# One combined first transfer, a new written-out order of steps, and half of the last V spread issued by ScalarE, in a two-block transformer kernel

## The chip, the core and the metric

One NeuronCore of a Trainium2 chip runs the whole kernel. It has five engines with a queue each: TensorE (PE in the profile; PEld is its weight load), VectorE (DVE), ScalarE (ACT), GpSimd (POOL) and SyncE (SP), which here only issues transfers. The metric is device microseconds of one execution, as a median over runs.

## What is computed

The reference runs two blocks one after the other on x of 32 batches x 32 tokens x 128 features, all in fp32:

```
cmod = silu(c) @ w_ada + b_ada        # 6 blocks: shift, scale, gate; twice
x_mod = ln(x) * (1 + scale) + shift;  k, q, v = split(x_mod @ w_qkv)
w = softmax(q k^T / 8) per head (16 heads of 8);  x = x + gate * (w v @ w_proj + b)
x = x + gate2 * (gelu(x_mod2 @ w_mlp1) @ w_mlp2)          # layer 0, "mlp"
self = [x, q] @ W_self.T ;  label bias and penalty from adj (32 x 32 x 11 labels)
for d in (0, 1):  out += gat_attention(self, adj or adj^T)  # 16 heads, first 20 tokens as keys
return x + relu(self + out)                                # layer 1
```

## The kernel before

Tokens lie in 8 groups of 4 batches (128 rows). Layer 0 normalises and projects in five chunks (`CHUNKS`: groups 0; 1; 2-3; 4-5; 6-7), and everything behind it goes in four halves of 2 groups (`MIDS`). Attention goes by unit: 8 units of layer 0 (one per group) and 16 of layer 1 (group x direction; units 8 to 23). A unit passes these steps: `scores` (32 small products on TensorE), `badd` (layer 1: the bias, VectorE, L1503), `max` (L1513, L1517), `sub` (L746, L1528; for odd units of layer 1 on GpSimd), `turn` (transposes, L1167, L1170), `exp` (ScalarE, L1307, L1310), `values` (products with V, L1190, L1199), and for a pair of units `recip` and `mult` (VectorE, L1541, L1552). Layer 1 ends with `ya`, `yb`, `relu` (L755, L766, L1562) and `store`.

The order of all work is a list written out by hand or by a planner beforehand: `ORDER` holds 541 entries (stage, key). `ON` and `TAKE_ON` say which engine runs an entry; each engine runs its own entries strictly in the order of the list, and waits on semaphores for what an entry reads. `take` copies a product out of PSUM. `BANKS` gives every product its PSUM bank, and an entry also waits until the bank's last user has been read (`bank_freed`, L699). An attention unit keeps its scores in one of 4 slots, so `badd` of a unit waits for `turn` of the unit four places before it (L1504).

Places that the change and the prediction touch:

- Loads (`fetch`, L833). SP issues `cols` (51 small columns: the condition, the biases), x1, `ada0` (blocks 0 and 1 of w_ada), qkv, x2, x3, x4, `ada1` (blocks 2 to 5) and the rest; ACT issues x0. `HOLD` makes a fetch wait until another has landed (`ada1` for `ada0`).
- Start. `warm` are products of ones with ones on TensorE that no one reads: 8, then 3 more behind `cmod 0`. `silu` (L1276) reads `cols`, `cmod 0` (L1026) reads silu's result and `ada0`. `masks` on VectorE reads `ident` of GpSimd; `plus1` on GpSimd reads `cols`.
- ScalarE loads a table when its function changes between Exp and Gelu. In the old order all 16 takes of `mlp1` (Gelu, L1239) lie between `exp` of unit 6 and `exp` of unit 11.
- `spread ('v1', m)` (L898): V of half m goes by 8 SBUF to SBUF transfers to the layout that `values` wants, all issued by SP. `values` waits for all 8.

Of the kernel before, what the change touches and what calls it, by code (L numbers as in the profile page):

```python
# [152 lines left out]
BANKS = {('warm', ('w0', 8)): 0,  # L153
 ('cmod', 0): 4,
 ('warm', ('w1', 3)): 5,
 ('xnT', 0): 0,
# [44 lines left out]
 ('turn', 7): 2,
 ('bias', 0): 3,
 ('bias', 1): 3,
 ('yT', 0): 1,
# [1 line left out]
 ('x1tok', 0): 1,
 ('xn2T', 0): 4,
 ('mlp1', 0, 0): 1,
 ('mlp1', 0, 1): 6,
# [1 line left out]
 ('mlp1', 0, 3): 6,
 ('mlp2', 0): 6,
 ('self', 0): 5,
 ('selfT', 0): 5,
 ('x2tok', 0): 2,
 ('k1', 0, 0): 2,
 ('q1', 0, 0): 0,
 ('k1', 0, 1): 7,
 ('q1', 0, 1): 2,
 ('v1', 0, 0): 6,  # L220
 ('v1', 0, 1): 3,
# [10 lines left out]
 ('yT', 1): 2,
 ('proj', 1): 2,
 ('x1tok', 1): 4,
 ('xn2T', 1): 2,
 ('mlp1', 1, 0): 2,
 ('mlp1', 1, 1): 2,
# [1 line left out]
 ('mlp1', 1, 3): 7,
 ('mlp2', 1): 2,  # L240
 ('self', 1): 1,
 ('selfT', 1): 1,
 ('x2tok', 1): 1,
 ('k1', 1, 0): 3,
 ('q1', 1, 0): 3,
 ('k1', 1, 1): 0,
 ('q1', 1, 1): 2,
 ('v1', 1, 0): 1,
 ('v1', 1, 1): 2,
# [1360 lines left out]
```

How the kernel before makes its waits and increments, by code:

```python
        def shift(engine, name, p):  # L721
            g0, g1 = MIDS[p]
            bs = slice(g0 * UB, g1 * UB)
            for s in fresh(name, ("take", (("xn2T", p), 0)), ("take", (("cmod", 1), 0))):
                engine.wait_ge(*s)
            return engine.tensor_tensor(xm[:, bs, :], xm[:, bs, :], over_s(cmod, 3, bs), ALU.add)
# [1 line left out]
        def resid(engine, name, which, m):  # L728
            g0, g1, bs = batches("mid", m)
            if which == 1:
                for s in fresh(name, ("xb", 0), ("take", (("proj", m), 0))):
                    engine.wait_ge(*s)
            else:
                for s in fresh(name, ("resid1", m), ("take", (("mlp2", m), 0)), ("dense", ("x1tok", m))):
                    engine.wait_ge(*s)
            return engine.tensor_tensor(xT[:, bs, :], gated[:, bs, :], xT[:, bs, :], ALU.add)
# [1 line left out]
        def subtract(engine, name, n):  # L738
            if layer_of(n):
                for s in fresh(name, ("badd", n), ("max", n)):
                    engine.wait_ge(*s)
            else:
                for s in fresh(name, ("copy", n), ("max", n)):
                    engine.wait_ge(*s)
            e = e_of(n)
            return engine.tensor_tensor(e, e, nm_of(n).unsqueeze(2).broadcast_to(list(e.shape)), ALU.add)
# [1 line left out]
        def add_dirs(engine, name, g):  # L748
            n = UNITS.index((1, 1, g))
            for s in fresh(name, ("mult", pair_of(n)), ("mult", pair_of(UNITS.index((1, 0, g))))):
                engine.wait_ge(*s)
            if g in SELF_FIRST:
```

## Time and profile before

| | us |
|---|---|
| median of 3 runs | 91.72 (91.64 to 93.18) |
| the profiled execution, its own time | 91.11 |
| its span, first to last instruction | 89.4 |
| PE busy | 79.5 (89%) |
| DVE busy | 68.4 (76%) |
| POOL busy | 57.7 (65%) |
| ACT busy | 51.1 (57%) |

Busy time of an engine is a share of the whole span; which engine holds the end up differs by stretch. In the chain of work that ended last PE has 72%, DVE 13%, POOL 5% and issue 5%. The granted TensorE clock was 0.989 of full speed as a mean, and 1.00 in every stretch read below.

### The profile page before, as it was taken

The numbers are of one execution on the slowest core, as the hardware profiler recorded it, in microseconds if no ns is written. First come the engines' busy times: TensorE is split into PE (matmuls) and PEld (weight loads), VectorE is DVE, ScalarE is ACT, GpSimd is POOL, SyncE is SP. The second block draws the span as 40 slices with busy tenths as digits, with TensorE's granted clock in tenths as the row PEclk, the third lists the DMA queues.
The fourth block names the chain that finished last, engine by engine and source line by source line (L and its number), as shares of the span: only waits on it lengthen the run. The fifth ranks groups of instructions, "written<-read, shape, count | busy, mean of one in ns | idle before, by whom it ended". The sixth has DMA issues, their size and how long they took to land.

```text
span 89.4 us, 4174 instructions
## 1 busy us (share of the span) xinstructions
PE 79.5 (89%) x1768; PEld 61.0 (68%) x1768; DVE 68.4 (76%) x203; ACT 51.1 (57%) x114; POOL 57.7 (65%) x82
## 2 busy tenths in 40 slices
PE   5997999998999899999999999999989969976810
PEld 5997757655666777878987766778777746645700
DVE  0679899799798865779262699299979997898870
...
GB/s 25 242 235 187 248 223 226 310 209 214 127 29 65 166 22 0 0 0 7 0 0 31 40 23 0 17 53 16 13 15 50 29 6 8 46 33 73 0 141 42
DMA packets 7076, 7.08 MB, mean 79 GB/s; under 512 B 1169, under 2 KB 6193, under 8 KB 7057
## 3 DMA queue, kind: packets, MB, share of 16 engines
...
## 4 chain that ended last, share of the span: by engine, by line
PE 72%; DVE 13%; issue 5%; POOL 5%; ACT 1%; DVEq 0%; POOLq 0%; ACTq 0%
PE ps_all L1155 11%; PE ps_all L1076 8%; PE ps_all L1082 8%; PE ps_all L1056 6%; PE ps_all L1000 6%; PE ps_all L1167 5%; PE ps_all L1119 4%; PE ps_all L1170 4%; PE ps_all L1104 4%; PE ps_all L1106 3%; PE ps_all L1199 2%; PE ps_all L1190 2%; DVE E L1503 2%; PE ps_all L1109 2%; PE ps_all L1064 2%
## 5 line engine op out<-in xcount | busy, mean ns | idle before, releaser
L1307 ACT ACTIVATE PT<-ps_all 120x384 f32<-120x384 f32 x16 | 7.5, 489 | 7.3 <-PE ps_all L1167 7.3
L785 POOL TENSOR_TENSOR Kb<-k_raw,head_mask 128x640 f32<-128x640 f32 x4 | 5.0, 1253 | 7.0 <-ACT Kb L1256 4.3
L1239 ACT ACTIVATE hidden<-ps_all,cols 128x256 f32<-128x256 f32 x16 | 7.1, 475 | 3.7 <-PE ps_all L1076 3.7
L1076 PE MATMUL ps_all<-xm,w_rest_sb 128*128 128x256 f32 x32 | 9.1, 387 | 0.0
L966 POOL TENSOR_TENSOR rstd<-var_eps,minus_half 128x2 f32<-128x2 f32 (+1 forms) x9 | 6.0, 665 | 4.7 <-DVE var_eps L1344 4.5
L736 POOL TENSOR_TENSOR xT<-gated,xT 128x256 f32<-128x256 f32 x8 | 5.8, 729 | 4.9 <-DVE gated L1391 3.9
L746 POOL TENSOR_TENSOR E<-E,neg_max 128x320 f32<-128x320 f32 x8 | 6.1, 771 | 3.5 <-DVE neg_max L1513 3.5
L1167 PE MATMUL ps_all<-ident,E 128*120 128x128 f32 x48 | 8.1, 284 | 0.2
L1056 PE MATMUL ps_all<-xm,w_qkv_sb 128*128 128x256 f32 (+1 forms) x30 | 7.5, 360 | 0.5 <-DVE xm L1371 0.5
L1190 PE MATMUL ps_all<-Vz,PT 120*32 120x54 f32 (+1 forms) x384 | 6.2, 208 | 2.0 <-DMA Vz<-v_raw 0.9
L1190 PEld LDWEIGHTS ps_all<-Vz,PT 120*32 120x32 f32 (+1 forms) x384 | 5.2, 109 | 3.8 <-ACT PT L1307 1.3
L1082 PE MATMUL ps_all<-hidden,w_rest_sb 128*128 128x256 f32 x32 | 7.8, 386 | 0.0
L773 POOL TENSOR_TENSOR Kb<-gated,head_mask 128x1024 f32<-128x1024 f32 (+1 forms) x4 | 6.7, 1679 | 1.5 <-ACT gated L1224 1.5
L1155 PE MATMUL ps_all<-Kb,home_b 32*32 32x80 f32 x512 | 7.1, 240 | 0.7 <-issue 0.4
L1513 DVE TENSOR_REDUCE neg_max<-E 128x16 f32<-128x320 f32 x16 | 7.4, 476 | 0.2
L1256 ACT ACTIVATE Kb<-ps_all,bk_masked,head_mask 128x160 f32<-128x160 f32 x16 | 7.1, 490 | 0.7 <-PE ps_all L1106 0.7
L1517 DVE TENSOR_REDUCE neg_max<-ps_all 128x16 f32<-128x512 f32 x8 | 5.5, 691 | 1.8 <-PE ps_all L1155 1.5
L801 POOL MEMSET Vz<- 128x2592 f32 x3 | 6.8, 2257 | 0.0
L1155 PEld LDWEIGHTS ps_all<-Kb,home_b 32*32 32x32 f32 x512 | 3.9, 103 | 4.2 <-issue 2.6
L1082 PEld LDWEIGHTS ps_all<-hidden,w_rest_sb 128*128 128x128 f32 x32 | 5.9, 190 | 1.0
L1310 ACT ACTIVATE PT<-ps_all 128x512 f32<-128x512 f32 x8 | 4.5, 595 | 3.4 <-PE ps_all L1170 3.3
L746 DVE TENSOR_TENSOR E<-E,neg_max 128x320 f32<-128x320 f32 x8 | 6.2, 787 | 0.1
...
## 6 DMA issues: line engine op xcount, KB each, us to landing
...
w_rest_sb<-in_w_rest SPq DMA_DIRECT2D x1, 576.0 KB, 7.9
...
q_tok<-q_rows SPq DMA_DIRECT2D x4, 128.0 KB, 3.2
...
```

What stands on the lines that cost most here:

```text
L746: return engine.tensor_tensor(e, e, nm_of(n).unsqueeze(2).broadcast_to(list(e.shape)), ALU.add)
L801: return engine.memset(Vz1[:, m, :, :, :, :, :], 0.0)
L1056: return pe.matmul(ps[:, 0:n], w_qkv_sb[:, o:o + P], xm[:, bs, :], start=True, stop=True)
L1076: return pe.matmul(ps[:, 0:n], w_of(W_MLP1 + name[2]), xm[:, bs, :], start=True, stop=True)
L1082: ins = pe.matmul(ps[:, 0:n], w_of(W_MLP2 + j), hidden[:, slot_of(h), j, 0:n], start=(j == js[0]), stop=(j == js[-1]))
L1155: ins = pe.matmul(to[QUAD * b:QUAD * b + QUAD, j, :], qT, Kb, start=True, stop=True)
L1167: ins = pe.transpose(ps[0:KR, c * P:(c + 1) * P], E1[:, r, c * KR:(c + 1) * KR], ident[:, :])
L1190: ins = pe.matmul(ps[QUAD * b:QUAD * b + QUAD, o + c * SIX * CW:o + c * SIX * CW + w], PT[0:n, key % RING, c, b * S:(b + 1) * S], V, start ...
L1239: return act.activation(hidden[:, slot_of(h), j, 0:n], ps[:, 0:n], ACT.Gelu_apprx_tanh, bias=cols[:, R_MLP1 + j:R_MLP1 + j + 1])
L1256: return act.activation(kb1_of(h, d)[:, part, :, :], ps[:, 0:nb * M].rearrange("p (b k) -> p b k", k=M), ACT.Identity, bias=bk_masked[:, d ...
L1307: ins = act.activation(PT[0:KR, key % RING, 0:CH, :], ps[0:KR, 0:CH * P].rearrange("p (j t) -> p j t", t=P), ACT.Exp)
L1513: ins = dve.tensor_reduce(nm_of(key), e_of(key), AX.X, ALU.max, negate=True)
```

## The change

Seven edits, of which the order is by far the longest.

```diff
+V_PARTS = [[(i, i, 0, CH, 0) for i in range(HI)],
+           [(i, (i - HI) * 2 + c, c, c + 1, CH) for i in range(HI, SIX) for c in range(2)]]
-HOLD = {'ada1': 'ada0', ...
+HOLD = {'ada1': 'cols', ...
+ ('spread', ('v1', 3, 1)): 'act',
- ('fetch', 'x1'): 'sp',
- ('fetch', 'ada0'): 'sp',
+ ('fetch', 'x1'): 'act',
-        cols = sb("cols", [P, COLS])
+        first = sb("first", [P, COLS + ADA_PARTS[0][1] * P])
+        cols = first[:, 0:COLS]
-        w_ada_sb = sb("w_ada_sb", [P, 6 * P])
+        w_ada_sb = sb("w_ada_sb", [P, (6 - ADA_PARTS[0][1]) * P])
...
             if what == "cols":
-                to, of = cols[:, :], cols_dram
+                to, of = first[:, :], cols_dram
...
+        def spread(engine, name, key):
...
+            m, part = key[1:]
...
+            for i, quad, c0, c1, j in V_PARTS[part]:
+                to, of = slice(M * i, M * i + M), slice(QUAD * quad, QUAD * quad + M)
+                engine.dma_start(Vz1[to, k, i, c0:c1, 0:nb, :, :]..., v1_raw[of, j:j + c1 - c0, bs, :, :]...)
...
-                        for s in fresh("pe", ("spread", ("v1", m))):
+                        for s in fresh("pe", *[("spread", ("v1", m, part)) for part in range(len(V_PARTS))]):
```

- `cols` and the first two blocks of w_ada arrive as one transfer (25.5 + 128 KB); `ada0` is gone, `ada1` waits for the combined one, and ACT issues x1 behind x0.
- The 8 transfers of `spread ('v1', m)` become two entries of 4. SP issues them all but the second of the last half, which ACT issues.
- `warm` is 7 products in one place instead of 8 + 3.
- `BANKS` is assigned anew, and all of `ORDER` is another sequence of the same steps (543 entries). Units of layer 0 now begin with group 0. The steps' engines are the same, but for x1 and the one spread.

The new order begins so:

```diff
+ORDER = [('zero', 'ones'), ('fetch', 'x0'), ('zero', 'v0_ones'), ('ident', 0), ('masks', 0), ('fetch', 'cols'),
+         ('stats', (0, 0)), ('consts', 0), ('fetch', 'qkv'), ('plus1', 0), ('rstd', (0, 0)), ('apply', 0),
+         ('fetch', 'x1'), ('silu', 0), ('warm', ('w0', 7)), ('zero', 'vz0b'), ('dense', ('cmod', 0)),
+         ('dense', ('xnT', 0)), ('stats', (0, 1)), ('take', (('cmod', 0), 0)), ('fetch', 'x2'),
+         ('take', (('xnT', 0), 0)), ('dense', ('k', 0)), ('dense', 'vsh'), ('dense', ('v', 0)), ('dense', 'qb'),
...
```

The long list is easier read by engine. These are entries of single engines, taken out of `ORDER` in their sequence, where the prediction speaks of them:

```
SP, start     before  cols x1 ada0 qkv x2 x3 x4 ada1 rows rest0 adj2 spread(v,1) rest1 ...
              after   cols qkv x2 ada1 x3 x4 rest0 rest1 xT spread(v,0) adj2 ...
DVE, start    before  ones stats0 stats1 masks apply0 nmr1 take cmod0 stats2 take xnT0 take xnT1 stats3 ... max 1
              after   ones masks stats0 apply0 stats1 take cmod0 take xnT0 stats2 stats3 nmr1 nmr2 take q0 ... max 0
PE, first scores of layer 1
              before  ... self 1, q1(0,0), mlp2 2, selfT 1, q1(0,1), xn2T 3, scores 8
              after   ... x2tok 0, v1(0,0), self 1, mlp1(2,0), mlp1(2,2), scores 8, selfT 1, mlp1(2,3) ... mlp2 2 ...
PE, around mlp2 3
              before  mlp2 3, scores 13, turn 10, ... q1(2,0), values 9, values 8, scores 18, turn 14, self 3, turn 15
              after   turn 15, mlp2 3, scores 19, values 8, values 9, scores 17, self 3, turn 13, q1(2,0)
ACT, middle   before  mlp1(3,3) k1 q1 mlp1(3,2) mlp1(3,0) mlp1(3,1) selfT 2, exp 11 8 9 10, k1(2,1) k1(2,0) ...
              after   k1(1,1), exp 11 10 9 8, selfT 2, mlp1(3,0) mlp1(3,1) k1(2,1) mlp1(3,2) k1(2,1) mlp1(3,3)
                      q1(2,1) k1(2,1) k1(2,0) k1(2,1), exp 15 13 ...
ACT, end      after   exp 19, exp 18, take q1(3,0), spread(v1,3,1), x2tok 3, exp 16, x2tok 2, exp 21, x2tok 1,
                      exp 20, exp 22, exp 23
PE, end       before  scores 23, x2tok 1, turn 21, values 18, turn 20, values 19 20 21, turn 22, turn 23, values 22 23
              after   scores 20, x2tok 3, turn 21, turn 23, x2tok 2, x2tok 1, values 17 16, turn 20, turn 22,
                      values 21 20 22 23
```

## Rows read from the trace of the kernel before

**Rows 1.** Busy time by stretch (us): PE, PEld, DVE, ACT, POOL, granted clock, DMA.

```profile
12.00:28.00 16.00, 15.43 (x443) 10.21 (x445) 14.05 (x37) 8.88 (x16) 11.14 (x17) 1.00 0.65 179
31.30:49.20 17.90, 17.90 (x169) 14.62 (x174) 10.79 (x40) 12.62 (x31) 12.01 (x13) 1.00 0.03 7
57.00:65.50 8.50, 8.43 (x257) 6.60 (x257) 6.89 (x16) 6.23 (x13) 4.22 (x6) 1.00 0.13 26
65.50:86.60 21.10, 16.70 (x571) 12.08 (x569) 19.29 (x51) 10.08 (x24) 12.16 (x21) 1.00 0.16 40
```

**Rows 2.** The chain of work that ended last: start us, us, what.

```profile
1.12 3.78 PE ps_all L1119 x16
...
46.62 1.73 PE ps_all L1082 x8
48.34 0.22 PE ps_all L1000 x2
...
49.21 0.35 PE ps_all L1155 x27
...
52.97 0.43 PE ps_all L1076 x2
...
60.04 0.47 PE ps_all L1167 x3
...
63.80 0.66 PE ps_all L1190 x48
64.46 0.37 PE ps_all L1155 x27
...
86.29 0.29 DVE x_tok L1562
```

**Rows 3.** Timeline of the start: start us, us, engine, line, what.

```profile
2.65 1.38 SPq L857 DMA_DIRECT2D x_tok<-in_x_tok  x3
...
2.93 0.29 DVE L1339 BATCH_NORM_STATS2 stats<-x_tok 128x6 f32<-128x128 f32 x1 [1.87 <-DMA x_tok<-in_x_tok]
...
4.70 0.34 DVE L1462 SCALAR_TENSOR_TENSOR xn_tok<-x_tok,meanvar,rstd 128x128 f32<-128x128 f32 x1
...
10.61 0.69 DVE L1517 TENSOR_REDUCE neg_max<-ps_all 128x16 f32<-128x512 f32 x1
```

**Rows 4.** DMA issues: what, queue, count, KB each, median us from issue to landing.

```profile
w_rest_sb<-in_w_rest SPq DMA_DIRECT2D x1, 576.0 KB, 7.9
...
x_tok<-in_x_tok SPq DMA_DIRECT2D x3, 128.0 KB, 2.8
...
w_qkv_sb<-in_w_qkv SPq DMA_DIRECT2D x1, 192.0 KB, 2.5
...
w_ada_sb<-in_w_ada SPq DMA_DIRECT2D x1, 128.0 KB, 2.2
...
cols<-in_cols SPq DMA_DIRECT2D x1, 25.5 KB, 1.9
```

**Rows 5.** Timeline, where `badd` of unit 18 begins; idle time before it in brackets.

```profile
65.52 0.49 DVE L1503 TENSOR_TENSOR E<-ps_all,bias_q 128x320 f32<-128x320 f32 x1 [0.41 <-PE ps_all L1167]
```

**Rows 6.** Timeline of ScalarE between 50 and 60 us.

```profile
50.63 0.85 ACT L1256 ACTIVATE Kb<-ps_all,bk_masked,head_mask 128x160 f32<-128x160 f32 x2
...
54.42 0.84 ACT L1239 ACTIVATE hidden<-ps_all,cols 128x256 f32<-128x256 f32 x2 [0.87 <-PE ps_all L1076]
...
57.54 1.28 ACT L1307 ACT_TABLE_LOAD   x1
...
58.83 1.25 ACT L1307 ACTIVATE PT<-ps_all 120x384 f32<-120x384 f32 x3
```

**Rows 7.** The layer 1 spread: its issues by line (ns, min/median/max), and who waited behind it.

```profile
L898 SPq DMA_DIRECT2D Vz<-v_raw x32: 706/766/1001, 46.2 to 80.2; - x32
...
82.20 0.73 PE L1190 MATMUL ps_all<-Vz,PT 120*32 120x54 f32 x48 [0.86 <-DMA Vz<-v_raw]
...
82.99 0.36 DVE L1541 RECIPROCAL rden<-ps_all 128x32 f32<-128x32 f32 x1 [0.53 <-PE ps_all L1190]
```

More of the change, by code:

```diff
@@ L199 @@
- ('values', 4): 2,
+ ('turn', 6): 0,
+ ('values', 4): 1,
  ('scores', 7): 4,
[L201 to L204, printed above, removed]
+ ('turn', 7): 4,
+ ('bias', 0): 0,
+ ('bias', 1): 2,
+ ('yT', 0): 2,
  ('proj', 0): 0,
[L206 to L209, printed above, removed]
+ ('x1tok', 0): 3,
+ ('xn2T', 0): 3,
+ ('mlp1', 0, 0): 6,
+ ('mlp1', 0, 1): 0,
  ('mlp1', 0, 2): 5,
[L211 to L221, printed above, removed]
+ ('mlp1', 0, 3): 2,
+ ('mlp2', 0): 2,
+ ('self', 0): 3,
+ ('selfT', 0): 3,
+ ('x2tok', 0): 7,
+ ('k1', 0, 0): 0,
+ ('q1', 0, 0): 4,
+ ('k1', 0, 1): 3,
+ ('q1', 0, 1): 5,
+ ('v1', 0, 0): 1,
+ ('v1', 0, 1): 1,
  ('scores', 8): 4,
- ('turn', 8): 1,
- ('values', 5): 6,
+ ('turn', 8): 3,
+ ('values', 5): 3,
  ('scores', 9): 4,
- ('turn', 9): 2,
+ ('turn', 9): 0,
  ('scores', 10): 4,
- ('turn', 10): 3,
@@ L229 @@
- ('values', 6): 3,
+ ('turn', 10): 2,
+ ('values', 6): 0,
  ('scores', 11): 4,
  ('turn', 11): 3,
[L232 to L237, printed above, removed]
- ('mlp1', 1, 2): 6,
[L239 to L249, printed above, removed]
+ ('yT', 1): 0,
+ ('proj', 1): 0,
+ ('x1tok', 1): 3,
+ ('xn2T', 1): 3,
@@ L281 @@
[L281 to L305 removed]
+ ('xn2T', 2): 7,
@@ new lines @@
+ ('mlp1', 2, 0): 3,
+ ('mlp1', 2, 1): 2,
+ ('mlp1', 2, 2): 1,
+ ('mlp1', 2, 3): 3,
+ ('mlp2', 2): 3,
+ ('self', 2): 1,
+ ('selfT', 2): 1,
+ ('x2tok', 2): 4,
+ ('k1', 2, 0): 4,
+ ('q1', 2, 0): 1,
+ ('k1', 2, 1): 3,
+ ('q1', 2, 1): 1,
+ ('v1', 2, 0): 6,
+ ('v1', 2, 1): 5,
+ ('scores', 16): 4,
+ ('turn', 16): 0,
+ ('values', 9): 6,
+ ('scores', 17): 4,
+ ('turn', 17): 0,
+ ('scores', 18): 4,
+ ('turn', 18): 3,
+ ('values', 10): 3,
+ ('scores', 19): 4,
+ ('turn', 19): 1,
+ ('yT', 3): 5,
+ ('proj', 3): 0,
@@ L306 @@
+ ('x1tok', 3): 0,
+ ('xn2T', 3): 2,
+ ('mlp1', 3, 0): 2,
+ ('mlp1', 3, 1): 1,
+ ('mlp1', 3, 2): 6,
+ ('mlp1', 3, 3): 7,
+ ('mlp2', 3): 2,
+ ('self', 3): 0,
+ ('selfT', 3): 0,
+ ('x2tok', 3): 2,
+ ('k1', 3, 0): 1,
+ ('q1', 3, 0): 0,
+ ('k1', 3, 1): 2,
+ ('q1', 3, 1): 3,
+ ('v1', 3, 0): 3,
+ ('v1', 3, 1): 4,
  ('scores', 20): 4,
  ('turn', 20): 4,
- ('values', 11): 4,
+ ('values', 11): 0,
  ('scores', 21): 4,
```

416 lines of the change are left out of this document (190 added, 226 removed), and 5 rows, old and new, of the table ORDER.

## The prediction, made before the changed kernel was run

> **What bounds the kernel now.** I read the busy time by stretch first, then the chain of waits, then the timeline where the chain changes engine. By stretch [rows 1] three regimes show. From 12 to 28 us VectorE is busy 14.05 of 16 us and TensorE 15.43: layer 0's attention feeds itself through max and sub, and both engines are close to full. From 31.3 to 49.2 us TensorE is busy all 17.90 us and VectorE 10.79: the mlp is TensorE's alone. From 65.5 to 86.6 us it is turned round, VectorE 19.29 of 21.10 and TensorE 16.70. The chain [rows 2] says the same: TensorE holds it through the middle, VectorE's last relu (86.29 + 0.29 = 86.58 us) ends it, and the store takes what is left to 89.4. So a microsecond of TensorE's work saved in the last stretch is worth nothing there; what counts is when VectorE can begin its last block of work, and whether it is kept fed. That block begins at 65.52 us with badd of unit 18 [rows 5], and it is 49 entries of the list long. In the new order exactly the same 49 entries stand from badd of unit 19 on. That makes the comparison simple: when does badd 19 begin, and does the block take less than its 86.58 - 65.52 = 21.1 us?
>
> **The change part by part.**
>
> *Combined transfer, x1 on ScalarE, warm.* The small columns took 1.9 us, 128 KB of w_ada 2.2 and 192 KB of w_qkv 2.5 [rows 4]. 153.5 KB lie between the last two; I take 2.4, so columns and w_ada land at 0.8 + 2.4 = 3.2 us. silu follows, and cmod is hidden behind the warm products: 14 instead of 16 instructions of 3.78 / 16 = 0.24 us [rows 2], to 4.4 us. What counts in the start is VectorE, and its chain is as before: stats of x0 at 2.93, apply at 4.70 [rows 3]. GpSimd's rstd now stands behind plus1, which waits for the larger transfer, at 3.2 plus 0.2: still before the statistics are ready. x0 now shares the engines with six times the bytes: the cost lies between 0 and the 0.6 us by which 192 KB took longer than 25.5 (2.5 against 1.9); I take 0.1. ScalarE issues x1 instead of SP: x1 then starts where it did, and delays only silu's table load, which has until 3.2 us.
>
> *Start order.* SP now issues ada1, held until 3.2 us, ahead of x3 and x4. x3 was issued at about 3.1 (the second of three in 1.38 us from 2.65 on, 0.46 each [rows 3]); now at about 3.7. With 2.8 us [rows 4] it lands at 6.5, and later by what ada1's 256 KB take away. By my adding up of its list VectorE comes to it at 6.9 us, because stats 3 now stands ahead of nmr 1, nmr 2 and take q0: if x3 is late, all of layer 0's start is. Then VectorE has to reach its first max: 10.61 us before [rows 3], with nearly equal work ahead of it (take v1, take q1 and an nmr less; take cmod1 and take v0 more). I add up 10.7 to 10.9. For the whole start I take +0.3 us; the bounds are -0.6 (masks, now done before x0 lands, stood between the first statistics and apply, and took about a third of the 1.77 us from 2.93 to 4.70) and +0.9 (x3 waits for all of ada1). qrow needs the second part of w_rest, issued at 3.2 + 4 x 0.46 = 5.0 us; with 7.9 us [rows 4] it lands at 12.9, and TensorE asks at about 13.3, behind scores 1. I cost it at nothing; if it is late, turn 0 stands behind it, for up to 0.5 us. From there to the mlp the same work runs in another sequence, bound by VectorE; I take nothing.
>
> *Layer 1 earlier.* Ahead of scores 8, which began at 49.21 [rows 2], TensorE no longer does mlp2 of half 2 (1.73 us), one mlp1 (0.43), selfT 1 and xn2T 3 (0.22 each), but x2tok 0 (0.22): 2.6 - 0.2 = 2.4 us less, all of it back-to-back work [rows 2]. Most is given back by scores 19: compared with scores 18 before, q1 (0.43) and two values (0.66 for both) are moved behind it, and turn 15 (0.47) and x2tok 0 (0.22) ahead of it, so only 1.09 - 0.69 = 0.4 us is left. Scores 18 began at 64.46, so scores 19 begins at 64.46 - 0.4 + 0.3 (start) = 64.4, and ends at 64.8. Before, scores 18 was done at 64.83, but badd 18 waited 0.41 us more, until 65.52, for turn 14, which stood behind it on TensorE and held its slot [rows 2, 5]. badd 19 needs turn 15, which now runs ahead of mlp2 3. So it begins at about 64.8: -0.7 us, start included.
>
> *ScalarE's two more tables.* The new order has exp 11, 10, 9, 8 ahead of the takes of mlp1 of half 3, and exp 15 behind them. Exp to Gelu to Exp: two table loads more than before. One took 1.28 us (57.54), and the next activation began 0.01 us behind it, at 58.83 [rows 6]. scores 19 needs four masked takes of k1(2,1), the last of which stands behind exp 8, selfT (0.47), a load (1.28), four mlp1 takes, four k1 takes, k1(2,0) and q1: ten at 0.42 in a row [rows 6]. exp 8 ends at about 57.9, so this is 57.9 + 0.5 + 1.3 + 4.2 = 63.9. The cover is TensorE's way to 64.4: 0.5 us of slack. The load before exp 15 hides behind scores 19 and values 8 and 9. Bounds: 0 and 2 x 1.28 = 2.57; I take +0.2, nearer to the cover. The Trainium skill (ScalarE: Activation LUTs, "What ACT_TABLE_LOAD costs") counts a drain as well, 2.66 us for a switch; the row shows no drain behind the load. By the page the sum would be some 1.4 us worse at this one place, and two switches are a rival below.
>
> *The last spread.* Eight issues at 0.77 us are 6.1 us of SP [rows 7]. The last of them ended at 81.0, and TensorE waited for the landing until 82.20, 0.86 us, while VectorE idled 0.53 us for the result [rows 7]. With four on each queue the issuing ends 3 us sooner; SP's half starts at the same place of VectorE's list. That frees 0.53 of VectorE; I take -0.4, bounds 0 and -0.86. The cost is 4 x 0.77 = 3.1 us of ScalarE's queue, ahead of x2tok 3, exp 16 and the last four exps. Counted back from VectorE's end, it stands at -10 to -7 us, exp 16 ends at -6, exp 20 and 22, which follow sub 20 and 22 at -5, have about 1 us to spare. So nothing, and up to +1 if take q1(3,0) comes late. The Trainium skill (DMA: Bandwidth & Descriptors, "Issuing engines are not separate DMA queues") says a second issuing engine saves only the issuing time, usually small beside the transfer. Here the rows make issuing the larger part; by the page's "small" this term would be 0.
>
> *Sum* against the profiled execution (span 89.4, own time 91.11): -0.7 + 0.2 - 0.4 = -0.9, so 90.2. The median shown is 0.6 above that execution; I carry this along: 91.72 - 0.9 = **90.8**.
>
> **The rivals.**
>
> *Everything comes through (22%).* The start gains its 0.6 instead of losing 0.3, and VectorE's 1.8 us of idle time in the last block [rows 1] falls to 1.0. That is -0.9 and -0.4 more: 89.5. For it speaks that x2tok and relu work has moved out of the last stretch's waits; against it, that layer 0's start is bound by VectorE, whose work is the same.
>
> *Nothing is gained (24%).* The gain at badd 19 is small and hangs on a place where TensorE, ScalarE and GpSimd (k1spread, resid2 and two memsets in line) all arrive within half a microsecond. One of them late by 0.8, or the split spread worth nothing, gives 91.4 to 92.0.
>
> *ScalarE becomes the bound between exp 11 and exp 15 (12%, the slower side).* Place: the takes of k1(2,1) ahead of scores 19, then exp 15. Price: two loads, 2.57 us, with the gain at badd 19 gone too: 91.72 + 2.57 - 0.4 = 93.9. It decides once exp 8 ends later than 58.4, 0.5 behind my count, and is complete if the Exp load also holds up values 13 and 12. Against it: ScalarE was busy only 6.23 of 8.5 us there [rows 1]. The page's 2.66 a switch, the rule named above, would give 5.3 us for two instead of 2.57, and a time of its own near 96; the row bears it out so little that it has 1 of these 12%.
>
> *The forecast (42%)* is the rest: 90.1 to 91.4.
>
> **How the numbers follow.** 2% is 1.8 us, about what a measurement of this kernel tells from no change: faster is below 89.9, slower above 93.6. Faster: the first rival, and a tenth of the forecast, 26%. Slower: most of ScalarE's case, 10%. Within: 64%. For the range I go to 89.2, which leaves a third of the first rival out, and up to 92.9, which takes the no-gain case whole with 0.9 for the start and leaves most of the slower case: 18% outside.
>
> **What would show it.** Right: badd 19 begins near 64.8 us and the block behind it takes under 21 us; the wait of 0.86 for the spread is gone; first max near 10.8; six table loads, none with TensorE idle behind it. Wrong: VectorE waits for x3 near 7 us; TensorE waits for a k1 take before scores 19; exp 16 or 20 late behind ScalarE's four issues.

## The result, and the profile after

The changed kernel took **96.57 us** (median of 4, 95.70 to 97.68), the kernel before beside it 92.45 (4 runs, 91.64 to 93.53): a ratio of 1.050, 95% interval 1.033 to 1.068. It is slower by 5%; the forecast was 90.8, with 92.9 as the upper end of the range. Executions of one kernel fall into a faster and a slower group, and every ratio with an interval here compares the faster ones alone (91.64 and 91.72 against 95.70, 96.11 and 97.03), while medians and ranges take in all, and of the profiled executions the changed kernel's, 97.68, is in the slower group, those of e19 and e20 in the faster.

The quickest comparison is by markers on VectorE: start of the first statistics, of the first, second and eighth `max` (the eight units of layer 0), of the first `badd` of layer 1, of the badd that opens the last 49 entries (18 before, 19 after), and the end of the last relu. E19 (all of the new order, without the three smaller costs) and e20 (the old list up to entry 176, then the new one) are experiments told below; the argument rests on them where they differ from the changed kernel's.

| us | before | after | order alone (e19) | old start, new rest (e20) |
|---|---|---|---|---|
| first statistics | 2.9 | 4.3 | 3.0 | 3.0 |
| first max | 10.6 | 13.3 | 12.4 | 11.1 |
| second max | 13.1 | 16.9 | 15.9 | 13.6 |
| eighth max | 27.8 | 32.5 | 31.6 | 28.5 |
| first badd of layer 1 | 49.8 | 51.5 | 50.7 | 48.8 |
| last block begins | 65.5 | 69.1 | 68.3 | 66.5 |
| last relu ends | 86.6 | 93.2 | 91.1 | 91.5 |
| own time | 91.11 | 97.68 | 95.24 | 95.33 |

So the changed kernel is 4.7 us late at the eighth max, wins back 3.0 before layer 1, gives back 1.8 as counted, and loses 3.0 in the last block: +6.6 in this execution, the longest of its four. In e19 the same three steps are +3.8, -2.9 and +1.9, and the last block +1.7.

Busy time by stretch, to set beside [rows 1] (same columns; the last two are the stretches that end and begin with the last block):

```profile
12.00:28.00 16.00, 15.45 (x345) 11.06 (x345) 14.19 (x33) 7.86 (x17) 10.63 (x15) 0.90 0.57 150
60.60:69.10 8.50, 8.45 (x200) 6.89 (x202) 6.90 (x16) 7.39 (x15) 4.87 (x5) 1.00 0.12 24
69.10:93.20 24.10, 18.35 (x617) 14.18 (x605) 18.91 (x51) 10.13 (x25) 12.54 (x21) 0.93 0.12 30
```

From 12 to 28 us both engines are as busy as before, but TensorE does 345 matmuls in 15.45 us instead of 443 in 15.43: it is slower, not idler. In the last block VectorE is busy 18.91 us for the same 51 instructions that took 19.29, in a stretch 3 us longer: it waits. VectorE and GpSimd at the start, against [rows 3]:

```profile
4.34 0.29 DVE L1350 BATCH_NORM_STATS2 stats<-x_tok 128x6 f32<-128x128 f32 x1 [1.89 <-DMA x_tok<-in_x_tok]
...
5.63 2.02 POOL L807 MEMSET Vz<- 128x2304 f32 x1
5.71 0.35 DVE L1473 SCALAR_TENSOR_TENSOR xn_tok<-x_tok,meanvar,rstd 128x128 f32<-128x128 f32 x1 [0.68 <-POOL rstd L974]
6.52 0.15 DVE L1355 TENSOR_SCALAR var_eps<-meanvar 128x1 f32<-128x1 f32 x1
...
8.81 2.06 DVE L1355 TENSOR_SCALAR var_eps<-meanvar 128x2 f32<-128x2 f32 x1
8.83 2.02 POOL L805 MEMSET Vz<- 128x2304 f32 x1
8.89 1.99 DVE L1467 SCALAR_TENSOR_TENSOR nmr<-meanvar,rstd 128x1 f32<-128x1 f32 x2
9.03 1.85 DVE L1386 TENSOR_TENSOR selfT<-ps_all,qb 128x128 f32<-128x128 f32 x1
...
13.31 0.68 DVE L1528 TENSOR_REDUCE neg_max<-ps_all 128x16 f32<-128x512 f32 x1
```

x0 lands 1.4 us later than before. `var_eps`, a VectorE instruction of 0.2 us, lasts 2 us, as long as GpSimd's memset beside it, and the `nmr` and `selfT` that follow it end only behind it. The memset at 5.63, just as long, holds nothing: a `var_eps` of one column beside it takes 0.15 us. So it is not any two instructions side by side. In the 20 kept traces, 40 times a TENSOR_SCALAR of two or more columns, from SBUF to SBUF, starts beside a memset of 2 us, and all 40 end 0.02 to 0.15 us behind it; no other VectorE instruction is held but behind one of these, `nmr` by itself 18 times in 0.15 to 0.16 us. (That agrees with the Trainium skill, SBUF — State Buffer, "SBUF: two separate sides", by which one of the two engines can block the other for a whole instruction.) TensorE in the same stretch:

```profile
6.21 0.30 PE L1008 MATMUL ps_all<-ident,xn_tok 128*128 128x128 f32 x1 [0.86 <-DVE xn_tok L1473]
7.28 0.49 PE L1064 MATMUL ps_all<-xm,w_qkv_sb 128*128 128x128 f32 x2 [0.77 <-DVE xm L1382]
8.58 1.76 PE L1034 MATMUL ps_all<-silu_c,w_ada_sb 128*128 128x32 f32 x8
11.04 0.74 PE L1163 MATMUL ps_all<-Kb,selfT 32*32 32x128 f32 x32 [0.71 <-issue]
```

It idles 0.86 and 0.77 us, and from 8.4 us the granted clock is 0.50, the lower of its two levels (1.2 instead of 2.4 GHz), until 15.2: the 8 matmuls of `cmod 1` take 1.76 us. The third wait, 0.71 us, is called "issue" by the profile, but `scores 0` reads `selfT`, which the held instruction kept back to 10.88. And TensorE in the last block:

```profile
70.63 0.27 PE L1175 MATMUL ps_all<-ident,E 128*120 128x128 f32 x1
71.60 0.38 PE L1175 MATMUL ps_all<-ident,E 128*120 128x128 f32 x2 [0.70 <-issue]
...
74.75 0.54 PE L1114 MATMUL ps_all<-selfT,w_rest_sb 128*128 128x160 f32 x2
76.77 0.69 PE L1117 MATMUL ps_all<-selfT,w_rest_sb 128*128 128x160 f32 x2 [1.48 <-issue]
```

"issue" says that nothing the profile shows held it up. Twice TensorE stops in the middle of a step, once between two of its three transposes. Behind the second stop the clock is 0.50 again, from 76.7 to 80.1 us. Now what was forecast at the opening of the block and at ScalarE's part of the spread:

```profile
69.11 0.49 DVE L1514 TENSOR_TENSOR E<-ps_all,bias_t 128x320 f32<-128x320 f32 x1
...
82.44 3.58 ACTq L884 DMA_DIRECT2D Vz<-v_raw  x4
86.17 0.38 ACT L1273 ACTIVATE home_b<-ps_all 128x256 f32<-128x256 f32 x1 [3.32 <-PE ps_all L1008]
```

### The profile page after: what moved, and what is told of

The parts are those of the page before. It is cut to its first block, busy times and chain, and to the rows that moved or that the text cites. A ratio compares the mean times of both kernels' runs of the same rounds, so it can differ in the third digit from the quotient of the medians.

```text
span 95.7 us, 4162 instructions
## 1 busy us (share of the span) xinstructions
PE 82.0 (86%) x1760; PEld 62.8 (66%) x1760; DVE 73.4 (77%) x203; ACT 53.0 (55%) x116; POOL 58.0 (61%) x82
## 4 chain that ended last, share of the span: by engine, by line
PE 57%; DVE 27%; issue 6%; DMA 4%; ACT 2%; POOL 1%; DVEq 0%; ACTq 0%; POOLq 0%
PE ps_all L1163 10%; PE ps_all L1008 6%; PE ps_all L1084 6%; PE ps_all L1064 6%; PE ps_all L1090 5%; PE ps_all L1175 5%; DMA x_tok<-in_x_tok 4%; PE ps_all L1178 3%; DVE E L755 3%; PE ps_all L1114 3%; DVE nmr L1467 2%; PE ps_all L1198 2%; DVE E L1514 2%; PE ps_all L1117 2%; PE ps_all L1207 2%
## 5 line engine op out<-in xcount | busy, mean ns | idle before, releaser
L745 POOL TENSOR_TENSOR xT<-gated,xT 128x256 f32<-128x256 f32 x8 | 6.3, 783 | 7.1 <-issue 3.5
L1064 PE MATMUL ps_all<-xm,w_qkv_sb 128*128 128x256 f32 (+1 forms) x30 | 8.5, 411 | 0.8 <-DVE xm L1382 0.8
L1247 ACT ACTIVATE hidden<-ps_all,first 128x256 f32<-128x256 f32 x16 | 7.1, 477 | 1.8 <-PE ps_all L1084 1.7
L1064 PEld LDWEIGHTS ps_all<-xm,w_qkv_sb 128*128 128x128 f32 x30 | 5.6, 237 | 1.7 <-DVE xm L1382 1.0
L1175 PEld LDWEIGHTS ps_all<-ident,E 128*120 128x120 f32 x48 | 5.7, 142 | 1.7 <-issue 0.8
```

Of the source, the lines that this page charges most:

```text
L1064: return pe.matmul(ps[:, 0:n], w_qkv_sb[:, o:o + P], xm[:, bs, :], start=True, stop=True)
L1175: ins = pe.transpose(ps[0:KR, c * P:(c + 1) * P], E1[:, r, c * KR:(c + 1) * KR], ident[:, :])
L1247: return act.activation(hidden[:, slot_of(h), j, 0:n], ps[:, 0:n], ACT.Gelu_apprx_tanh, bias=cols[:, R_MLP1 + j:R_MLP1 + j + 1])
```

## The experiments

A pause is an "issue" wait of TensorE of over 0.3 us, other than the one for `selfT`. "Before" is the kernel before, run in the same comparison.

### First comparison (before: 93.74, 91.6 to 94.69)

**E1, columns apart.** The changed kernel, with the transfer taken apart.

```diff
-HOLD = {'ada1': 'cols', ...
+HOLD = {'ada1': 'ada0', ...
+ ('fetch', 'ada0'): 'sp',
...
```

> The changed kernel with one edit undone: the small columns come alone again, and blocks 0 and 1 of w_ada as a second transfer behind them; order, banks and x1 on ScalarE stay. Theory A (the large first transfer delays x0): x0's statistics begin at 2.9 to 3.2 us instead of 4.34, the first max comes 1 to 2.5 us sooner than 13.31, TensorE's clock at 1.2 GHz between 8.4 and 15 us is shorter or absent, and the kernel comes out 1.5 to 3 us faster than the changed one (some 93.5 to 95). Theory B (the order is what costs, not the transfer): x0's statistics come sooner, but the first max stays near 12.5 or later because VectorE is held at 8.8 us for the 2 us of GpSimd's memset, and the time changes by under 0.8 us.

Measured: 95.59 (95.42 to 95.95), 1.040 of before (1.033 to 1.047). Statistics begin at 2.98 us, first max at 11.9 instead of 13.3, but the second at 15.7 and the eighth at 31.3. The combined transfer does delay x0, here by 1.3 us. Between the medians lies 1 us, but the two intervals overlap, so 1 us is what it can have cost, not what it is shown to cost; most of the start's loss stays.

**E2, combined transfer alone.** The kernel before with the combined transfer, `x1` on ScalarE and `ada1` held by it.

```diff
-HOLD = {'ada1': 'ada0', ...
+HOLD = {'ada1': 'cols', ...
- ('fetch', 'x1'): 'sp',
- ('fetch', 'ada0'): 'sp',
+ ('fetch', 'x1'): 'act',
...
```

> The kernel before with one part of the change alone: the columns and blocks 0 and 1 of w_ada in one transfer, ada1 held by it, x1 issued by ScalarE; order, banks and warm products of before. Theory A: x0's statistics move from 2.93 to about 4.3 us, the first max from 10.61 to about 12, and the kernel is slower by 1 to 1.6 us (92.9 to 93.5). Theory B: the start has slack behind the warm products and the time stays within 0.5 us of before.

Measured: 94.35, but from 91.46 (granted clock 0.996 over the run) to 95.27 (0.945). The fastest is level with the fastest of before, 91.60, so no cost of the transfer by itself is shown. In the profiled one, 94.98, TensorE idles twice and then runs at half speed for 10 us, of which the column shows the first 8:

```profile
6.64 0.42 PE L1005 MATMUL ps_all<-ident,xn_tok 128*128 128x128 f32 x2 [0.78 <-ACT xn_tok L1288]
7.94 1.41 PE L1061 MATMUL ps_all<-xm,w_qkv_sb 128*128 128x128 f32 x5 [0.73 <-DVE xm L1376]
...
8.00:12.00 4.00, 4.00 (x20) 4.00 (x21) 2.08 (x12) 1.99 (x8) 2.87 (x5) 0.50 0.65 219
12.00:16.00 4.00, 4.00 (x44) 2.82 (x45) 1.98 (x5) 1.54 (x5) 0.73 (x3) 0.50 0.52 154
```

64 matmuls in 8 us, where the kernel before does 142. The first max comes at 13.7, the second at 18.1 and the eighth at 31.9, 3 to 5 us late, with the old order throughout. x0's delay of 0.7 us becomes a gap of TensorE, and behind the gap comes the low clock. It isn't the only thing that spreads this kernel's times: one execution took 93.72 at a clock of 0.998.

**E3, spread alone.** The kernel before, with the last V spread split and ScalarE's half behind `exp 18`.

```diff
+ ('spread', ('v1', 3, 1)): 'act',
...
```

> The kernel before with one part alone: the last V spread in two entries of four transfers, the second issued by ScalarE behind exp 18. By my prediction's step the wait of 0.86 us of TensorE for this spread is gone and the time falls by 0 to 0.5 us. Rival: the four issues (3.1 us or, as in the changed kernel's trace, 3.6 us on ScalarE's queue) push exp 21 and exp 20 back and the time rises by 0.5 to 1.5 us.

Measured: 94.64 (94.25 to 97.56), 1.027 (1.018 to 1.035). An exp waited for ScalarE's four issues:

```profile
83.93 3.60 ACTq L879 DMA_DIRECT2D Vz<-v_raw  x4
87.63 0.87 ACT L1313 ACTIVATE PT<-ps_all 120x384 f32<-120x384 f32 x2 [3.38 <-issue]
```

In the old order the split gains nothing and costs some 2 us. The profiled execution, the slowest, also shows pauses of 1.26 and 2.01 us near 18 and 25 us, so not all of its length is the spread's.

**E4, no more tables.** The changed kernel, with Identity for Gelu in the last half's takes (that half's mlp is not the reference's).

```diff
-   ... ACT.Gelu_apprx_tanh,
+   ... ACT.Identity if h == 3 else ACT.Gelu_apprx_tanh,
```

> The changed kernel without its two additional table loads: the four takes of mlp1 of the last half apply the identity instead of Gelu (so this part of the mlp is not computed as the reference has it), which costs the same per instruction (0.47 us) and needs no other table. If ScalarE's tables cost time, the kernel is 0.5 to 2.6 us faster than the changed one. If they are hidden, as the trace suggests (mlp2 of the last half begins at 66.7 us right behind TensorE's other work), it is within 0.5 us of it.

Measured: 97.48 (97.14 to 98.24), 1.061 (1.051 to 1.071), no less than the changed kernel. Its trace has 4 table loads where the changed kernel's has 6, and no gain is seen from that.

### Second comparison (before: 91.38, 90.57 to 93.18)

**E5, memsets moved.**

```diff
-         ('fetch', 'x1'), ('silu', 0), ('warm', ('w0', 7)), ('zero', 'vz0b'), ...
-         ('zero', 'vz0a'), ('dense', ('xnT', 2)), ...
+         ... ('fetch', 'qkv'), ('zero', 'vz0b'), ('plus1', 0), ...
+         ('fetch', 'x1'), ('silu', 0), ('warm', ('w0', 7)), ('zero', 'vz0a'), ...
```

> The changed kernel, with GpSimd's two memsets of 2.02 us in other places: vz0b into GpSimd's idle time ahead of plus1, vz0a behind the first rstd; nothing lies between 6.8 and 8.8 us any more where VectorE's nmr and var_eps were 1.99 and 2.06 us long. Theory (VectorE is held while GpSimd's memset writes): those two fall to under 0.5, the first max comes 1.0 to 2.0 us sooner than 13.31, and the median falls by 0.5 to 1.5 from 96.6, to 95.1 to 96.1. Rival (they waited for data, and the memset only ended at the same time): the first max stays at 13.0 to 13.3 and the median at 96.6. Second rival (the clock of 0.50 from 8.45 to 15.1 us sets the start): first max sooner by under 0.5, median the same.

Measured: 96.50 (95.77 to 97.77), 1.059 (1.049 to 1.070). The mechanism is as expected:

```profile
8.05 0.17 DVE L1355 TENSOR_SCALAR var_eps<-meanvar 128x2 f32<-128x2 f32 x1
8.13 0.22 DVE L1467 SCALAR_TENSOR_TENSOR nmr<-meanvar,rstd 128x1 f32<-128x1 f32 x2
...
11.29 0.68 DVE L1528 TENSOR_REDUCE neg_max<-ps_all 128x16 f32<-128x512 f32 x1
```

The first max comes 2.0 us sooner, but the second only 1.1 (15.8), at a granted clock of 0.50 from 8 to 12 us, and the time does not move. The memset that now begins at 1.74 holds `masks`, TENSOR_SCALARs of four columns, for 1.58 us instead, to 3.78; in e10 and e19 it reaches the first statistics too, which take 0.8 us.

**E6, more warm products.**

```diff
+ ('warm', ('w1', 3)): 7,
+ ('warm', ('w2', 4)): 7,
...
-('dense', ('cmod', 0)), ('dense', ('xnT', 0)),
+('dense', ('cmod', 0)), ('warm', ('w1', 3)), ('dense', ('xnT', 0)), ('warm', ('w2', 4)),
```

> The changed kernel with seven more products of ones in TensorE's gaps at 5.4 and 6.5 us (3 behind cmod 0, 4 behind xnT 0). Theory (the gaps are what the clock fell behind): the granted clock stays at 1.00 through 8 to 15 us, scores 0 takes half as long, the first max comes by 12 instead of 13.31, and the median falls by 1 to 2, to 94.6 to 95.6. Rival A (the clock falls all the same, as the whole start is thin in products): 0.50 in the same stretch, median 96.6. Rival B (layer 0's start is bound by VectorE, whatever the clock): clock 1.00 but first max within 0.5 of 13.3. The seven products also move every later product on by 14 instructions with their weight loads: if TensorE's pauses with no wait behind them (at counts 1226 and 1352 of its matmuls) hang on the place in the instruction stream, they come at the same count of all matmuls, 7 places earlier in the work; if on a step of the work, at 1233 and 1359.

Measured: 99.87 (the profiled one), 96.15, 98.24 and 92.84 (granted clock 0.984 in the last). TensorE first, and then its count of matmuls up to each of two pauses:

```profile
8.04 0.98 PE L1036 MATMUL ps_all<-silu_c,w_ada_sb 128*128 128x32 f32 x8
10.43 0.51 PE L1165 MATMUL ps_all<-Kb,selfT 32*32 32x128 f32 x32 [1.42 <-DVE selfT L1388]
...
0.00:72.85 72.85, 64.66 (x1227) 50.19 (x1227) 55.90 (x156) 43.54 (x93) 48.12 (x65) 0.98 0.32 84
0.00:80.10 80.10, 70.42 (x1352) 54.94 (x1352) 59.04 (x165) 45.74 (x98) 50.63 (x69) 0.96 0.30 79
```

The filled gaps held the clock (`cmod 1` in 0.98 us), until TensorE idled 1.42 us behind VectorE's held instructions; the clock fell later instead (0.60 from 12 to 16 us), and the first max came at 12.6, the second at 16.5: the theory's 12 and 94.6 to 95.6 were missed. Its part on the clock is borne out; that the start is won by it is not, as the one fast execution has no trace. And with 14 matmuls more ahead of them, the pauses (1.99 and 1.49 us) still come at counts 1227 and 1352: in the changed kernel it is 1226 and 1352. They hang on the place in the instruction stream, not on a step; they now cut `scores` in two.

**E9, spread back on SP.**

```diff
- ('spread', ('v1', 3, 1)): 'act',
```

> The changed kernel with all 8 transfers of the last V spread issued by SP again, nothing else changed. Theory (ScalarE's 3.58 us of issuing holds up x2tok 3 and exp 16 and costs about what it cost alone, 94.64 against 93.74): the last block, from badd 19 to the last relu, falls from 24.06 us by 1 to 2.5, the median to 94.5 to 95.5. Rival (the block is long because TensorE pauses and the clock falls at 76.8 us, ScalarE had slack): the median stays within 0.4 of 96.6. Prediction's reading (the split saves 0.4): it becomes 97.

Measured: 97.83 (96.66 to 98.09), 1.067 (1.058 to 1.076). The theory fell; by the number it lies beyond both other readings (96.6 and 97), and its interval overlaps the changed kernel's, so whether the split saved anything is not shown. For the rival speaks that the block takes 24.1 us either way, and that in both traces TensorE, not ScalarE, releases the home_b behind the issues.

**E10, order alone.** E1's, e5's and e9's edits together.

> The changed kernel with three costs taken out together: small columns and blocks 0 and 1 of w_ada as two transfers, the memsets moved, the last spread on SP alone. What is left of the change is the order, with x1 issued by ScalarE and the warm products in one place. If the three are what made it slower (first theory): 96.6 - 1.0 - 1.0 - 1.5 = 93, level with the kernel before (93.7 in the last comparison). If the order itself costs (its steps follow each other so that TensorE pauses or waits at 68 to 80 us): 94.5 to 95.5, with the pauses near counts 1226 and 1352 still there. If the order saves what I forecast, 0.7 at badd 19: 92.8 or less.

Measured: 95.85 (95.44 to 97.33), 1.046 (1.039 to 1.053). The first theory fell. Nearly the whole loss is in the order (with x1 on ScalarE and the warm products in one place, which no run takes out by themselves).

### Third comparison (before: 93.65, 90.67 to 97.78)

**E13, old start, new rest.** `ORDER` = the old list's first 176 entries, then what is left in the new list's sequence.

> The list of the kernel before up to its entry 176 (all of layer 0's attention but the last steps), and from there what is left in the sequence of the changed kernel; transfers as before, the last spread on SP. Theory (the new start costs 2.8 us by the second max and 3.6 by the eighth; the rest is good but for TensorE's pauses without a wait): eighth max at 28 us as before, the first badd of layer 1 about 19 us behind it (22.0 before, 19.0 in the order alone), at 47, badd 19 at 64.5, the last relu between 85.5 (no pause) and 88.5 (pauses of 3 us in all): 0.97 to 1.01 of the kernel before. Rival (the rest is what costs): 1.03 or more, with the block from badd 19 on over 23.5 us. If the pauses hang on the place in the instruction stream, they come at counts 1226 and 1352 of TensorE's matmuls again, 4 products later in the work than in the changed kernel.

Measured: 92.76 to 98.17, median 95.11, too far apart for a verdict; e20 is the same kernel again. The first badd came at 49.2, not 47, and the pauses at counts 344 (1.14 us), 1350 (1.36) and 1604 (0.62).

**E14, new start, old rest.** `ORDER` = the new list's first 178 entries, then the old sequence; three banks changed.

> The reverse: the changed kernel's list up to its entry 178, with its combined transfer and x1 on ScalarE, and from there what is left in the sequence of the kernel before (3 PSUM banks reassigned, so that nothing waits for itself). Theory (the start is most of the loss): eighth max at 31.5 to 32.5 us, all behind it as before but 4 to 4.5 later, block of the last 49 entries near 21.5: 1.035 to 1.05 of the kernel before. Rival (the new rest makes the loss): within 1.5% of the kernel before.

Measured: 97.65 (96.97 to 98.18), against a kernel before that ranged from 90.67 to 97.78 in this comparison: 1.04 of its median and 1.08 of its fastest, with no interval to give. Eighth max at 33.4, everything up to the last block as far apart as before, and no pause. But the last block took 23.3 us, not 21.5: TensorE waited for the spread, longer than the 0.86 of [rows 7], and went on at half speed (48 matmuls in 1.19 us, 0.73 before):

```profile
88.25 1.19 PE L1207 MATMUL ps_all<-Vz,PT 120*32 120x54 f32 x48 [1.54 <-DMA Vz<-v_raw]
```

**E12, scores 1 early** (on the order alone).

```diff
-('dense', ('k', 2)), ('dense', ('q', 2)), ('dense', ('v', 2)), ..., ('dense', ('xnT', 3)), ('scores', 1),
+('scores', 1), ('dense', ('k', 2)), ('dense', ('q', 2)), ('dense', ('v', 2)), ...
```

> The order alone (small columns and w_ada apart, memsets moved, last spread on SP), with scores 1 ahead of k, q and v of the third group pair on TensorE instead of behind them and behind xnT 3; nothing else. Theory (VectorE stands idle before the second max because TensorE does those products of some 0.33 us each first): the second max comes 1.5 us sooner than 15.9, at 14.0 to 14.6, the eighth max 0.8 to 1.5 sooner than 31.4, and the time falls by as much against 95.85. Rival (scores 1 waits for kspread 1 or for q's take anyway, or the products only move to stand in front of scores 2): second max sooner, eighth max at 31 to 31.5, time the same within 0.4.

Measured: 99.46 (97.87 to 103.75): worse. TensorE now waited 0.99 us for `sub 0`, with the products behind it late, and max 1 had been left behind them in VectorE's list: second max 17.7. There are also pauses of 1.47, 1.36 and 1.76 us, so not all of the loss is the edit's. The edit was half an edit; e15 makes it whole.

**E11, small spreads** (on the order alone).

```diff
-to, of = slice(M * i, M * i + M), slice(QUAD * quad, QUAD * quad + M)
+to, of = slice(M * i, M * i + 2), slice(QUAD * quad, QUAD * quad + 2)
```

> The order alone again, but each of the 32 transfers of layer 1's V spreads carries 2 of its 20 rows (the values of layer 1 lack the rest): as many issues, a tenth of the bytes and packets. Theory (TensorE's pauses of 1.08 and 1.10 us at 70 and 75 us come because its next block of instructions is fetched behind the spreads' packets): both pauses fall under 0.4 and the block from badd 19 to the last relu falls from 23.7 by about 2 us; 93.5 to 94.5. Rival (the fetch is late whatever else the DMA engines do, as they are only some 10% busy there): pauses of 0.7 to 1.5 us at the same counts 1226 and 1352, time within 0.7 of 95.85.

Measured: 96.33 (96.08 to 97.0), pauses of 0.72 and 1.49 us at the same counts. The spreads' bytes have no part in them.

### Fourth comparison (before: 92.81, 92.04 to 94.63)

**E15 and E18, the two units together** (on the order alone).

```diff
-('sub', 0), ('fetch', 'rest1'), ('dense', ('k', 2)), ('dense', ('q', 2)), ('dense', ('v', 2)), ('take', (('q', 2), 0)),
+('sub', 0), ('fetch', 'rest1'), ('dense', ('k', 2)), ('scores', 1), ('max', 1), ('dense', ('q', 2)),
+('dense', ('v', 2)), ('take', (('q', 2), 0)), ('sub', 1),
...
```

> The order alone once more, with scores 1 behind the product k 2 on TensorE, and this time max 1 and sub 1 moved ahead in VectorE's list too (max 1 behind sub 0, sub 1 behind take q 2); the run with scores 1 alone moved left max 1 where it was, behind take q 2 and take xnT 3, and lost. Theory (the start of the new order is slow because the work of the next groups, 12 products on TensorE and two takes on VectorE, stands between the first two units): second max at 13.5 to 14.2 instead of 15.9, eighth max sooner than 31.4 by 0.8 to 1.5, the time 94.4 to 95.2 where the order alone had 95.85. Rival (what is moved behind scores 1 is only late next, kspread 2 and scores 2): second max at 13.5 to 14.2, but the third at 18 as before, time unchanged within 0.4.

Measured: 95.76, 96.13 and 98.8, and a profiled execution of 140.95 us, in which everything was slow and which shows nothing of the start; e18 is the same kernel again.

**E16, the kernel before with more warm products.**

```diff
-('warm', ('w1', 3)), ... ('dense', 'qb'),
+('warm', ('w1', 5)), ... ('dense', 'qb'), ('warm', ('w2', 2)),
```

> The kernel before, with two more products of ones behind cmod 0 (5 instead of 3) and two behind qb, in TensorE's gap of 0.55 us ahead of v 1. Theory (the kernel before is spread from 90.67 to 97.78 because the granted clock falls in some executions behind short gaps of its start): the runs lie closer together, granted clock 0.99 or more in most, median 0.3 to 1.5 lower than the kernel before in the same comparison. Rival (the clock falls for another reason): same spread, median the same within 0.5. Cost if the products come in the way: 4 x 0.24 = 1 us of TensorE, of which 0.55 lies in the gap: up to 0.4 slower at the first max.

Measured over 10 runs: 92.65 (90.96 to 94.5), 0.998 (0.992 to 1.003). The rival held, the spread is the same: the profiled execution, at a clock of 1.00, had pauses of 1.12 and 0.68 us, at counts 344 and 1607. There is no version here that beats the kernel before.

**E17, few spread issues** (on the order alone).

```diff
-for i, quad, c0, c1, j in V_PARTS[part]:
+for i, quad, c0, c1, j in V_PARTS[part][:1 if m < 3 else HI]:
...
```

> The order alone, with one transfer in place of four in each part of the spreads of halves 0, 1 and 2 of layer 1 (values of layer 1 then lack most of V; what is not written holds ones): 6 issues instead of 24, SP idle for most of 60 to 80 us. Theory (TensorE's next block of instructions is asked for late, 2.5 to 2.9 us behind the start of the block, because SP's issues of 0.77 us stand in a row at that time): its 16 KB packet comes 0.7 to 1 us behind counts 1100 and 1226, the pauses at counts 1226 and 1352 fall under 0.3, the block from badd 19 on is 1.5 to 2 shorter. Rival (issues have no part in it; the kernel before asks within 0.7 us at counts 1226 and 1352 in the middle of such a row): packets still 2 to 3 us late, pauses 0.7 to 1.5, block within 0.7 of the 23.7 of the order alone.

Measured: 95.7 (93.3 to 96.86). The rival held: the packets come 2.7 and 2.5 us behind the starts of their blocks, and TensorE still pauses twice:

```profile
70.45 0.38 PE L1177 MATMUL ps_all<-ident,E 128*120 128x128 f32 x2 [0.79 <-issue]
75.34 0.43 PE L1119 MATMUL ps_all<-selfT,w_rest_sb 128*128 128x160 f32 x2 [1.22 <-issue]
```

### Fifth comparison, 5 rounds (before: 91.67, 90.87 to 96.28)

> The order alone with scores 1, max 1 and sub 1 moved ahead, once more, since its profiled execution took 141 us and shows nothing of the start. Theory: second max 13.3 to 14.2 us where the order alone had 15.9, eighth max below 30.6, and 0.8 to 1.5 us less than the order alone beside it in this comparison. Rival: second max sooner, but the eighth at 31 to 31.5, and the same time as the order alone within 0.4.

Measured: e18 95.78 (94.74 to 96.72), 1.044 (1.036 to 1.051). The second max came at 14.0 instead of 15.9, the third at 18.2 as in e19, the eighth at 32.0, behind a pause of 0.85 us. The rival held: what is moved ahead is only late next, and the intervals of e18 and e19 overlap.

> The order alone, beside the two others in one comparison: 1.04 to 1.05 of the kernel before; second max at 15.9, eighth at 31.4 to 32.4; pauses of TensorE near counts 1226 and 1352, with the 16 KB packet of instructions 2.3 to 2.7 us ahead of the end of each pause.

Measured: e19 96.51 (95.24 to 97.48), 1.055 (1.048 to 1.062), pauses of 0.99 and 1.22 us at counts 1226 and 1352, and one of 0.40 at 345.

> Old start and new rest once more, as its four times lay between 92.76 and 98.17. Theory (the new start is two thirds of the loss): 1.01 to 1.02 of the kernel before and 2.5 to 3.5 us less than the order alone beside it; from badd 19 on 20 to 21 us plus its pauses. Rival (the rest is the loss as much as the start): within 1.5 us of the order alone.

Measured: e20 95.94 (94.91 to 100.64), 1.042 (1.035 to 1.048). The theory's 1.01 to 1.02 fell. The start was won, 3.1 us at the eighth max, and lost again to pauses. First e19's start, then e20's, then e20's last block:

```profile
8.77 1.75 PE L1036 MATMUL ps_all<-silu_c,w_ada_sb 128*128 128x32 f32 x8
11.97 3.13 PE L1066 MATMUL ps_all<-xm,w_qkv_sb 128*128 128x128 f32 x12
```

```profile
9.09 0.98 PE L1049 MATMUL ps_all<-silu_c,w_ada_sb 128*128 128x32 f32 x8
```

```profile
69.53 0.33 PE L1178 MATMUL ps_all<-Kb,home_b 32*32 32x80 f32 x4 [2.02 <-issue]
...
75.28 0.34 PE L1178 MATMUL ps_all<-Kb,home_b 32*32 32x80 f32 x8 [1.64 <-issue]
...
83.96 0.25 PE L1178 MATMUL ps_all<-Kb,home_b 32*32 32x80 f32 x1 [0.91 <-issue]
```

E19's `cmod 1` took 1.75 us, as in the changed kernel at a granted clock of 0.50; the column shows 1.00 for that stretch, for which the trace has no record of the clock (its first is at 13.9 us), and here the durations are the better witness. They say a little more: in e19, as in e9, e11 and e14, they are doubled from the first matmul to 14 us or later. There the clock did not fall behind the gaps; it had not risen before.

## Where the pauses come from

The profile's table of queues lists one for TensorE's instructions: 13 packets, 0.21 MB, so 16 KB each. Between two neighbouring pauses lie 126 or 127 matmuls and as many weight loads, with a few other instructions (counts seen: 218, 344, 471, 1226, 1352, 1605, 1732). So one packet is one block of the instruction stream. The counts, and the packets in short windows, of the changed kernel (up to 66.50, up to the first pause's end at 71.59, up to the second's at 76.76; then 68.9 to 69.3):

```profile
0.00:66.50 66.50, 61.08 (x1100) 46.60 (x1101) 53.17 (x149) 40.26 (x87) 44.79 (x61) 0.95 0.34 91
0.00:71.59 71.59, 65.41 (x1226) 49.91 (x1227) 56.73 (x159) 43.58 (x93) 47.79 (x65) 0.95 0.32 86
0.00:76.76 76.76, 69.10 (x1352) 52.86 (x1353) 59.92 (x167) 47.16 (x102) 51.48 (x71) 0.95 0.31 82
```

```profile
q8 instruction: 1, 0.02, 19.2%
```

The packet moves at 69.1, the pause ends at 71.60. The other pairs: 74.4 and 76.77; in e10 68.25 and 70.85, 73.3 and 75.73; in e6 70.2 and 72.86, 77.4 and 80.11; in e20 66.9 and 69.53, 72.9 and 75.28. **Every one of these pauses ends 2.3 to 2.7 us behind a 16 KB packet.** Over all 20 kept traces there are 50 pauses, all at such counts; 49 end 2.2 to 2.9 us behind a packet, and one of 0.39 us ends 3.2 behind. TensorE passes count 1100 at 66.5, the packet comes 2.6 us behind, another 2.5 pass until it is in use, and TensorE has done its 126 matmuls in 4.4. Before, the packets come at 62.75, 67.05 and 71.1, within 0.6 to 0.9 us of the blocks' starts at 61.9, 66.3 and 70.4, and blocks of 4.1 to 4.4 us run through. (The Trainium skill, Runtime: NRT & Kernel Launch, "Instruction fetch mechanics", gives the same 16 KiB and 256 instructions and calls the cost mostly hidden; here it is up to 2.0 us.)

The rest of the order decides whether the two blocks of 66 to 77 us run through. Of the 15 traces with the new rest 13 pause at both borders, e13 at the second alone and e15, with everything slow, at neither; of the 5 with the old rest (before, e2, e3, e14, e16) none does. Elsewhere the old order pauses too, up to 2.01 us at count 344 in e3.

That the late packet holds TensorE up is a reading of these times; no run makes a packet come sooner. What makes the packet late is **open**. It is not the spreads' bytes (e11) nor SP's row of issues (e17; the kernel before issues spreads through both of its prompt packets at 67 and 71), not the table loads (e4 pauses as long, 1.35 and 1.49), not `mlp2` at the start of the block (before, a block begins with it at 57.7 and the packet comes at 58.55).

## Why the prediction was wrong

- **Combined transfer: mis-sized.** It said x0 would pay 0.1 us and at most 0.6, and the transfer itself 2.4. In the seven traces that have it, x0 takes 2.7 to 3.5 us to land (3.5 in the changed kernel) where the 13 others have 2.1 to 2.2: 0.6 to 1.4 us. The transfer takes 3.3 in the changed kernel. E1 puts the effect on the time at about 1 us at most. The bound came from the difference of two transfers that were not beside x0.
- **Start order, +0.3: the step that failed first.** Said +0.3 us for the whole start and at most +0.9, bound by VectorE, with nothing more up to the mlp; measured at the eighth max +4.7, and +3.8 in e19. Its count of VectorE's work was right: first max at 10.7 to 10.9 said, 11.0 in e10, 10.9 in e18. What it left out is TensorE's own speed. It took two warm instructions less as time saved and had no term for the three later products; those stood in a gap, and the new list leaves 1.6 us of gaps at 5.4 to 7.3. Behind them the products run at 1.2 GHz. In e19 between 8 and 17 us that is, by my estimate from durations at either level, 0.8 for `cmod 1`, 1.1 for nine small k, q, v matmuls and some 0.5 for the rest, 2.4 us, nearly the 2.8 by which the second max is late. Another 1.0 us is lost from there to the eighth max, at full clock, and only 0.40 of it is a pause; the rest has no explanation. That the gaps bring the low clock is borne out from both sides, though by single traces: with the old order and later x0 it came (e2), with the new order and the gaps filled it stayed away until the next gap (e6). No run has the new start at full clock throughout, so the 2.4 us are argued, not shown. What held TensorE up was, beside x0, the `var_eps` that waited out GpSimd's memset, priced nowhere (e5).
- **x3 and qrow:** not late, as costed.
- **Layer 1 earlier: right.** Said 2.4 us less work ahead of the first badd and 2.0 of it given back. Measured from eighth max to first badd: 22.0 before, 19.0 after, 19.1 in e19, but 20.3 in e20; from there to the last block 15.8 before and 17.6 to 17.7 in all three. With +4.7 from the start instead of +0.3, badd 19 at 69.1 instead of 64.8 follows.
- **Two tables, +0.2:** no loss seen (e4). The wait of 1.28 us ahead of badd 19 is for TensorE's `mlp2 3`. The Trainium skill's 2.66 us a switch (ScalarE: Activation LUTs, "What ACT_TABLE_LOAD costs") is not seen.
- **Last spread, -0.4: not shown.** Its sign came true, TensorE's wait of 0.86 us for the spread is gone, but it is just as gone in e9, e10 and e19, where SP issues all eight: the order took it away, not the split. E3 is slower, and e9 settles nothing. The rule of the Trainium skill (DMA: Bandwidth & Descriptors, "Issuing engines are not separate DMA queues"), that a second issuing engine has little to gain, came nearer than my term.
- **Last block, 21.1 us or less: the second step that failed.** It assumed that VectorE bounds it. Its work indeed did not change: less the pauses, the block takes 21.06 - 0.38 = 20.7 us before, 22.8 - 2.2 = 20.6 in e19, 24.9 - 4.6 = 20.3 in e20; 24.1 - 2.2 = 21.9 in the changed kernel, with 3.4 us at half clock in it. The pauses were in the page of before, at 0.38 us in all, and I had no term for them.
- **The rivals.** The slower one put the place right, between exp 11 and exp 15 and behind it, and the cause wrong: ScalarE was not the bound. None had TensorE's clock or its instruction fetch in it, and so the range ended too low.

The two losses are shown separately and do not add up simply: e14 has the new start without pauses (eighth max at 33.4, 97.65 us in all), e20 the pauses without the new start (1.04 of before), and together they are 1.05.
